# Projection's input turned by VectorE and transfers, overlapping columns of local exponentials added by GpSimd, a new time table

## The reference, cut to what matters

```python
x = x + _layernorm(_L0_attn_ref(_layernorm(x), w_qkv, w_out, b_out))
x = x + _layernorm(_L0_ffn_ref(_layernorm(x), w_freq_real, w_freq_imag, bias))

def _L0_attn_ref(x, w_qkv, w_out, b_out):          # x (2, 8192, 512), 16 heads of 32, W = 64
    qkv = (x @ w_qkv).reshape(B, N, 3, H, Dh)
    # local: query q sees keys from q - 32 to q + 31; softmax over these; times v
    # global: all queries see the keys k[:, ::64] (128 of them); softmax; times v[:, ::64]
    return (out_local + out_global).reshape(B, N, C) @ w_out + b_out

def _L0_ffn_ref(x, w_freq_real, w_freq_imag, bias):
    y = real(ifft(fft(x) @ w))                     # the kernel makes one 512x512 matrix of it
    return y + bias
```

## Time and profile before

| | |
|---|---|
| time, median of 3 runs | 3613.41 us (3602.11 to 3613.45) |
| the profiled execution | 3610.1 us, its span 3608.4 us |
| mean granted clock of TensorE | 0.988 of full speed |
| busy: PE, PEld, DVE, ACT, POOL | 98%, 76%, 63%, 55%, 54% of the span |
| DMA | 571 MB, 158 GB/s over the span |

### The profile page before, as it was taken

One profiled execution on the slowest core, in us unless ns is written; L12 is line 12 of the kernel. 1 busy time (PEld: TensorE's weight loads), 2 busy tenths in 40 slices (PEclk: granted clock), 3 DMA queues, 4 the chain that ended last, 5 costly groups with the idle time before them and its releaser, 6 DMA issues.

```text
span 3608.4 us, 77520 instructions
## 1 busy us (share of the span) xinstructions
PE 3540.8 (98%) x28482; PEld 2753.2 (76%) x28482; DVE 2262.6 (63%) x4672; ACT 1977.4 (55%) x4132; POOL 1935.8 (54%) x3091
## 2 busy tenths in 40 slices
PE   8999999999999899999999999999999999999997
PEld 6888888888888677777777777777777777777775
DVE  4333333333333477777777777777777777777774
ACT  3222222222222467677667767677777777677764
POOL 0000000000000367787787877887777878887787
PEclk9999999999999699999999999999999999999999
DMA  4545545455457666666666666666666666666651
GB/s 151 210 157 192 188 161 209 163 186 195 154 198 217 132 138 152 159 152 143 156 156 157 155 146 154 160 152 143 153 158 155 150 151 151 161 156 146 151 125 42
DMA packets 420885, 571.22 MB, mean 158 GB/s; under 512 B 41656, under 2 KB 187208, under 8 KB 420568
## 3 DMA queue, kind: packets, MB, share of 16 engines
q1 hardware_dynamic: 412024, 564.79, 59.9%
q10 hardware_dynamic: 8256, 2.16, 0.3%
q0 software_dynamic: 288, 0.08, 0.0%
HBM read 361.59 MB, written 203.23 MB: 157 GB/s over the span
## 4 chain that ended last, share of the span: by engine, by line
PE 62%; POOL 1%; ACTq 0%; ACT 0%; issue 0%; DVE 0%; DMA 0%; POOLq 0%; SPq 0%; DVEq 0%
PE ps_misc L1058 19%; PE ps_sc L998 7%; PE ps_ml L974 7%; PE ps_o L1030 6%; PE ps_mg L979 5%; PE ps_s L1030 4%; PE ps_sc L1012 4%; PE ps_o L1042 3%; PE ps_s L1036 3%; PE ps_sc L1067 2%; PE ps_sc L985 1%; PE ps_sc L1006 1%; ACTq L841 0%; POOL rsb L751 0%; DMA w_both<-mt 0%
## 5 line engine op out<-in xcount | busy, mean ns | idle before, releaser
L886 DVE TENSOR_REDUCE mx<-ps_ml 128x2 f32<-128x384 f32 x1024 | 561.7, 549 | 390.8 <-PE ps_ml L974 390.0
L451 PE MATMUL po<-ht_hi,w_both 128*128 128x512 f32 x2048 | 654.2, 393 | 1.5 <-ACT ht_hi L276 1.5
L846 ACT ACTIVATE ps_ml<-mask 128x384 f32<-128x384 bf16 x1022 | 501.9, 491 | 206.3 <-DVE mx L886 128.7
L818 ACT ACTIVATE qk<-ps_sc 128x384 f32<-128x384 f32 (+1 forms) x1024 | 416.8, 458 | 221.0 <-PE ps_sc L998 219.2
L451 PEld LDWEIGHTS po<-ht_hi,w_both 128*128 128x128 f32 x2048 | 385.2, 188 | 81.1 <-ACT ht_hi L276 1.8
L760 POOL TENSOR_SCALAR_AFFINE_SELECT qk<-qk 128x512 f32<-128x512 f32 (+1 forms) x512 | 298.2, 582 | 247.1 <-ACT qk L818 246.1
L889 DVE TENSOR_REDUCE mx<-ps_mg 128x2 f32<-128x256 f32 x1024 | 425.2, 415 | 1.9 <-PE ps_mg L979 1.9
L451 PE MATMUL po<-ht_lo,w_both 128*128 128x512 f32 x1024 | 399.3, 390 | 0.0
L831 ACT ACTIVATE v<-ps_sc 128x512 f32<-128x512 f32 x512 | 304.8, 596 | 94.1 <-PE ps_sc L1012 88.5
L763 POOL TENSOR_SCALAR_AFFINE_SELECT qk<-qk 128x512 f32<-128x512 f32 x512 | 326.0, 637 | 35.0
L455 PE MATMUL po<-w_both,ht_hi 128*128 128x512 f32 x1024 | 332.7, 396 | 0.0
(11 more groups left out here) (161 smaller groups left out, 8194.4 us busy)
## 6 DMA issues: line engine op xcount, KB each, us to landing
w_both<-q_hi_d SPq DMA_DIRECT2D x256, 256.0 KB
ks<-k_hi_d SPq DMA_DIRECT2D x128, 288.0 KB
xb<-in_L_attn_x SPq DMA_DIRECT2D x132, 256.0 KB, 2.9
q_lo_d<-o_lo SPq DMA_DIRECT2D x32, 1024.0 KB, 8.7
k_lo_d<-o_lo SPq DMA_DIRECT2D x32, 1024.0 KB, 10.1
w_both<-q_lo_d SPq DMA_DIRECT2D x128, 256.0 KB
vw<-v_d SPq DMA_DIRECT2D x128, 256.0 KB, 3.0
out<-xb SPq DMA_DIRECT2D x128, 256.0 KB, 3.3
```

What stands on the lines that cost most here:

```text
L451: last = nc.tensor.matmul(po[o % 6][:], wa[:, k, o * P:(o + 1) * P], ha[u][:, k, :], start=start, stop=stop)
L818: nc.scalar.activation(p_loc[:, i, 2 * hp:2 * hp + 2, lo:MW], ps_sc[n % 2][:, 0:2 * MW].rearrange("p (h n) -> p h n", h=2)[:, :, lo:MW], A ...
L846: nc.scalar.activation(ps_ml[u % 2][:, :, 0:MW], mask[:].rearrange("p (o n) -> p o n", o=1).to_broadcast([P, 2, MW]), ACT.Copy).then_inc(s ...
L886: nc.vector.tensor_reduce(mx[s % 2][:, 0, heads, tile], ps_ml[u % 2][:, :, 0:MW], axis=AX.X, op=ALU.max).then_inc(ml_taken, 1)
```

## The change

In the projection, from the second chunk on, TensorE turns nothing any more. VectorE turns the 32x32 blocks of each normalized tile (`turn`) into `turned`, which uses the buffer `at`; 16 transfers issued by ScalarE ahead of output 3 (`move`, `MOVE` = 3), each from 32 partitions to 32 partitions and 64 KB in pieces of 512 B, bring the blocks to their places in `x_t`, which uses `bt`; ScalarE and VectorE split this ahead of outputs 7 and 8 (`split`). To make the blocks land in order, the tokens of a chunk are loaded interleaved (`load_x`, four transfers of 256 KB and not one of 1 MB). The outputs use eight PSUM banks in turn (`bank`) and not six. The first chunk is turned as before.

In the attention, GpSimd adds the last 64 queries of tile i - 1 and the first 64 of tile i for i = 1, 2, 3 into `p_sum`, each after its select. The products with ones are then made in `pvl` 1, 3 and 4 alone: for the columns that one tile fills from `p_loc`, for the others from `p_sum`. The local exponentials wait for the last product of their pair of tiles. The products with the values stay as they are. The numbers of the table are new, and `SEED` has eight values that differ.

```diff
@@ -75,6 +75,10 @@
...
+    BANKS = 8
+    BLOCKS = P // DH
+    MOVES = BLOCKS * BLOCKS
+    MOVE, SPLIT = 3, (7, 8)
...
@@ -96,8 +100,9 @@
...
-        pt = [ctx.enter_context(nc.psum_tensor(f"pt{i}", [P, KT, P], F32)) for i in range(2)]
-        po = [ctx.enter_context(nc.psum_tensor(f"po{i}", [P, D], F32)) for i in range(6)]
+        po = [ctx.enter_context(nc.psum_tensor(f"po{i}", [P, D], F32)) for i in range(BANKS)]
+        pt = [p[:].rearrange("p (a n) -> p a n", a=KT) for p in po[BANKS - 2:]]
+        turned, x_t = at[:].rearrange("p k (b t i) -> p (k b) t i", b=BLOCKS, t=TILES), bt
...
@@ -119,9 +124,12 @@
...
-        banks = [*(p[:].rearrange("p a n -> p (a n)") for p in pt), *(p[:] for p in po)]
...
+        banks = [p[:] for p in po]
...
+        bank = lambda o, u: (o + u * (NOUT + TILES)) % BANKS
+        x_rows = x.rearrange("b n d -> (b n) d")
...
@@ -143,6 +151,12 @@
...
+                def load_x(c, u):
+
+                    for a in range(BLOCKS):
+                        sp.dma_start(xb[u][a * DH:(a + 1) * DH, :, :],
+                                     x_rows[bass.ds(c * CHUNK + a * P, P), :].rearrange("(t i) d -> i t d", i=DH)).then_inc(x_loaded[u], 16)
+
...
@@ -176,9 +190,11 @@
                 def body(c, u, follow):
                     if follow == 2:
-                        sp.wait_ge(t_done, c * TILES + TILES)
-                        sp.dma_start(xb[u][:], x_v[:, bass.ds((c + 2) * TILES, TILES), :]).then_inc(x_loaded[u], 16)
-
+                        if isinstance(c, int) and c == 0:
+                            sp.wait_ge(t_done, TILES)
+                        else:
+                            sp.wait_ge(turn_done, c * TILES)
+                        load_x(c + 2, u)
                     sp.wait_ge(ev_act, c * (NOUT + TILES) + NOUT + TILES)
                     sp.wait_ge(ev_dve, c * NOUT + NOUT)
                     pad_at = c * CHUNK + (c // CPB) * (PSEQ - SEQ) + HALF
@@ -268,12 +284,26 @@
...
-                def t_evac(c, u, t):
-
-                    act.wait_ge(t_done, c * TILES + t + 1)
-                    if t == 0:
+                def first_hi(t):
+
+                    act.wait_ge(t_done, t + 1)
+                    nc.scalar.activation(ht_hi[0][:, :, t * P:(t + 1) * P], pt[t % 2], ACT.Copy).then_inc(t_hi, 1)
+
+                def move(c):
+
+                    act.wait_ge(turn_done, c * TILES)
+                    act.wait_ge(t_lo, c * TILES)
+                    for a in range(BLOCKS):
+                        for b in range(BLOCKS):
+                            act.dma_start(x_t[b * DH:(b + 1) * DH, :, a * P:(a + 1) * P],
+                                          turned[a * DH:(a + 1) * DH, b::BLOCKS, :, :].rearrange("j k t i -> j k (t i)")).then_inc(moved, 16)
+
+                def split(c, u, k):
+
+                    if k == 0:
+                        act.wait_ge(moved, c * (16 * MOVES))
                         at_least(act, mm_done, NOUT + TILES, c, -(NOUT + TILES))
-                    nc.scalar.activation(ht_hi[u][:, :, t * P:(t + 1) * P], pt[t % 2][:], ACT.Copy).then_inc(t_hi, 1)
+                    nc.scalar.activation(ht_hi[u][:, k, :], x_t[:, k, :], ACT.Copy).then_inc(t_hi, 1)
                 def body(c, u, follow):
@@ -281,11 +311,14 @@
                         act.wait_ge(stored[u], (c // 2) * 80)
                         act.wait_ge(kg_copied, c * 2 - 2)
                     for o in range(NOUT + TILES):
-                        if follow and o % 3 == 2:
-                            t_evac(c + 1, 1 - u, o // 3)
+                        if follow and o == MOVE:
+                            move(c + 1)
+                        if follow and o in SPLIT:
+                            split(c + 1, 1 - u, 2 * o - 2 * SPLIT[0])
+                            split(c + 1, 1 - u, 2 * o - 2 * SPLIT[0] + 1)
                         act.wait_ge(mm_done, c * (NOUT + TILES) + o + 1)
                         dst = o_hi[u][:, o, :] if o < NOUT else o_v[u][:, o - NOUT, :]
-                        nc.scalar.activation(dst, po[o % 6][:], ACT.Copy).then_inc(ev_act, 1)
+                        nc.scalar.activation(dst, po[bank(o, u)][:], ACT.Copy).then_inc(ev_act, 1)
                         if isinstance(c, int) and c == 0 and o < KT:
                             piece(2 * KT + o)
@@ -343,13 +376,23 @@
...
-                def t_evac(c, u, t):
-
-                    dve.wait_ge(t_hi, c * TILES + t + 1)
-                    if t == 0:
+                def first_lo(t):
+
+                    dve.wait_ge(t_hi, t + 1)
+                    nc.vector.tensor_tensor(ht_lo[0][:, :, t * P:(t + 1) * P], pt[t % 2], ht_hi[0][:, :, t * P:(t + 1) * P].bitcast(F32),
+                                            ALU.subtract).then_inc(t_lo, 1)
+
+                def turn(c, u, t):
+
+                    dve.wait_ge(xn_done, c * TILES + t + 1)
+                    nc.vector.transpose(turned[:, :, t, :], xb[u][:, t, :].rearrange("p (b i) -> p b i", i=DH)).then_inc(turn_done, 1)
+
+                def split(c, u, k):
+
+                    dve.wait_ge(t_hi, c * TILES + k + 1)
+                    if k == 0:
...
-                    nc.vector.tensor_tensor(ht_lo[u][:, :, t * P:(t + 1) * P], pt[t % 2][:],
-                                            ht_hi[u][:, :, t * P:(t + 1) * P].bitcast(F32), ALU.subtract).then_inc(t_lo, 1)
+                    nc.vector.tensor_tensor(ht_lo[u][:, k, :], x_t[:, k, :], ht_hi[u][:, k, :].bitcast(F32), ALU.subtract).then_inc(t_lo, 1)
...
@@ -367,17 +410,21 @@
                 def body(c, u, follow):
                     if follow:
+                        norm(c + 1, 1 - u, 0)
                         for t in range(TILES):
-                            norm(c + 1, 1 - u, t)
+                            if t + 1 < TILES:
+                                norm(c + 1, 1 - u, t + 1)
+                            turn(c + 1, 1 - u, t)
...
                         dve.wait_ge(stored[u], (c // 2) * 80)
                         dve.wait_ge(kg_copied, c * 2 - 2)
                     for o in range(NOUT + TILES):
-                        if follow and o % 3 == 2:
-                            t_evac(c + 1, 1 - u, o // 3)
+                        if follow and o in SPLIT:
+                            split(c + 1, 1 - u, 2 * o - 2 * SPLIT[0])
+                            split(c + 1, 1 - u, 2 * o - 2 * SPLIT[0] + 1)
                         if o < NOUT:
                             dve.wait_ge(ev_act, c * (NOUT + TILES) + o + 1)
-                            nc.vector.tensor_tensor(o_lo[u][:, o, :], po[o % 6][:], o_hi[u][:, o, :].bitcast(F32),
+                            nc.vector.tensor_tensor(o_lo[u][:, o, :], po[bank(o, u)][:], o_hi[u][:, o, :].bitcast(F32),
                                                     ALU.subtract).then_inc(ev_dve, 1)
...
@@ -424,11 +471,12 @@
...
-                def transposes(c, u, t):
-                    pe.wait_ge(xn_done, c * TILES + t + 1)
-                    at_least(pe, t_lo, TILES, c, t - 1)
+                def transposes(t):
+                    pe.wait_ge(xn_done, t + 1)
+                    if t > 1:
+                        pe.wait_ge(t_lo, t - 1)
...
-                        last = nc.tensor.transpose(pt[t % 2][:, k, :], xb[u][:, t, k * P:(k + 1) * P], ident[:])
+                        last = nc.tensor.transpose(pt[t % 2][:, k, :], xb[0][:, t, k * P:(k + 1) * P], ident[:])
...
@@ -438,8 +486,8 @@
...
-                        p = (o - 6) % (NOUT + TILES)
-                        off = 0 if o >= 6 else -1
+                        p = (o - BANKS) % (NOUT + TILES)
+                        off = 0 if o >= BANKS else -1
...
@@ -448,19 +496,16 @@
...
-                                    last = nc.tensor.matmul(po[o % 6][:], wa[:, k, o * P:(o + 1) * P], ha[u][:, k, :],
+                                    last = nc.tensor.matmul(po[bank(o, u)][:], wa[:, k, o * P:(o + 1) * P], ha[u][:, k, :],
...
-                                    last = nc.tensor.matmul(po[o % 6][:], ha[u][:, k, t * P:(t + 1) * P],
+                                    last = nc.tensor.matmul(po[bank(o, u)][:], ha[u][:, k, t * P:(t + 1) * P],
...
-                        if follow and o % 3 == 1:
-                            transposes(c + 1, 1 - u, o // 3)
-
...
-                        transposes(0, 0, t)
+                        transposes(t)
...
@@ -595,6 +640,7 @@
...
+        p_sum = qk0[:].rearrange("p a n -> p (a n)")[:, 16 * MW:16 * MW + 12 * WIN].bitcast(F32).rearrange("p (i h n) -> p i h n", i=3, h=4)
...
-        MAXIMA = (-12.805, -11.6121, -10.9287, -9.5739, -8.6889, -7.4926, -6.9092, -5.6717)
...
-        SEED = (0.7311, 0.7311, 0.7311, 0.7311, 0.7311, 0.7311, 0.7311, 0.7311)
-        SCORES = (("mt", 0, -4.1303), ("loc", 0, -0.7012), ("loc", 1, 0.756), ("loc", 2, 1.2851), ("loc", 3, 4.7272),
...
-        VALUES = (("pvl", 0, 3.7999), ("pvl", 1, 3.8198), ("pvl", 2, 6.7674), ("pvl", 3, 7.039), ("pvl", 4, 7.8708),
...
```

(42 more changed lines are left out.)

35 lines of the change are left out of this document (18 added, 17 removed).

## The result

3583.67 us, median of 6 runs (3579.64 to 3591.01), against 3612.97 us before (6 runs): 0.9924 of it, 95% interval 0.9908 to 0.9940. That is 29 us less, where 61 were forecast (3552 us). The profiled execution took 3585.8 us, with a span of 3584.1 us.

A forecast was written before the change was run, and what follows sets the result against it. TensorE was taken to bound both long stages. From 3610.1 us, 59 us less for the projection's transposes and 0 for the attention gave 3551, or 3554 from the median; stated 3552 us, with a range of 3508 to 3618.

The forecast's parts named there:

- What bounds the kernel: Both long stages: TensorE, busy in 98% of the span, sets the end; GpSimd has 2.73 us of waits per attention step.
- The transposes, 59 us: Projection: TensorE's transposes leave all chunks but the first, 31 x 1.9 = 59 us less, if delivery precedes the next chunk.
- The issues: Projection: ScalarE issues 16 transfers per chunk at 0.565 us each, 9.0 us, done at 17.2 us, at no cost.
- the 1.05 MB: Projection: extra transfer traffic per chunk, at 80 us of engine time per MB, 5.3 us on 16 engines, landing by 24.
- The 4.6 us in hand: Projection: turned tiles split and ready at 28 us into a chunk, needed at 32.6, so the move costs 0.
- TensorE's shorter sums, 0.24 us per step: Attention: products with ones fall from 1.32 to 1.08 us per step, 31 us over 128 steps; bounds nothing to 42 us.
- GpSimd's add, 0.70 us plus 0.1: Attention: each of three adds per step costs 0.70 us plus a 0.1 gap, 2.4 us, making GpSimd's own work 18.06.
- the attention's period, 18.39 us: Attention: leftover waits keep the step 0.24 us above TensorE's 18.15, the present period, giving back the 31 us; net 0.
- the rival "GpSimd sets the step": Attention: GpSimd's 18.06 us plus remaining waits set the step; with half the waits left, 3685 us in all; chance 22%.
- the point from which it decides: Attention: a step of 18.85 us, or 0.79 us of GpSimd waits, at which the projection's 59 us are used up.
- The table, 0: Attention order: new numbers move items by tenths of a unit, remove no work; 0, up to 20 us of range downwards.
- The rule for the add: Attention: the skill advises VectorE for two-input adds, GpSimd being about twice as slow; on VectorE about 1.1 us for three.

The follow-up runs named there:

- experiment 4: Changed projection, table as before: shorter sums without GpSimd's adds, 3508.83 us; three adds made and waited for but unused, sums as before, 3588.69 us.
- `MOVE` = 4: Changed projection with the attention and table of before, its 16 transfers issued ahead of output 4 instead of 3: 3546.91 us, against 3555.17.
- experiment 7: Changed projection, attention and table of before, transfers issued ahead of output 4 or 5: 3546.91 and 3549.36 us, against 3555.17 ahead of output 3.
- experiment 6: Changed projection, shorter sums, table as before: adds on VectorE 4056.21 us; instead only the small constant's addition there 3549.48; also a deviation operation, transfers later, 3649.34.
- the repaired kernel: The whole change with the table as before, the small constant added on VectorE, and transfers issued ahead of output 4: 3542.95 us.
- the one that leaves the idea out: Changed projection with transfers issued ahead of output 4, attention and table as before the change: 3546.91 us.

## Why the prediction was wrong, by its own steps

- **What bounds the kernel: right.** TensorE sets both stages before. With its part shortened and GpSimd's left alone (experiment 4) the step is 18.06 us, shorter by what the columns taken out come to.
- **The transposes, 59 us: right in the mechanism, 54 to 56 measured.** Some 0.15 us per chunk is lost at the chunk's start, and without it (`MOVE` = 4) the projection's last product stands 60.8 us earlier than before. Two terms under it were off. The issues take 0.96 us each and not 0.565, 15.4 us and not 9.0, since they fall among the stores (experiment 7); the forecast took the median of rows that reach to 1.584; and the 1.05 MB cost 90 us of engine time per MB, not 80 (the page's row of ScalarE's queue is now 34.70 MB at 5.4% of 16 engines). So the pieces are there at 28.7 us after the chunk's start and not at 24, all is split at 32.6 and not at 28. The 4.6 us in hand were not there with the transfers where they stood. That the 59 us came out all the same was luck: the last piece was split 4.6 us later than forecast, and the room was 4.6 us.
- **TensorE's shorter sums, 0.24 us per step: too small.** 0.33 measured, the upper bound by columns. I priced a group of 192 columns by one that another of its kind follows, 0.32 us; the next such group, which other work follows, took 0.44 (2405.70 to 2406.14 in the timeline). That this is the difference is likely, but no run singles it out.
- **GpSimd's add, 0.70 us plus 0.1: right**, 0.733 us and about 0.08. GpSimd's own work per step: 18.06 forecast, 18.04 measured.
- **The step that failed: the attention's period, 18.39 us.** "I expect some to stay: 0.24 us per step above TensorE's own". 0.58 us above it: 18.64, 128 x 0.25 = 31 us, of the 32 that the forecast missed. I treated GpSimd's 2.73 us of waits as room that an add could fill for nothing until it was full, and put the leftover at a value that made the sum zero. What the runs showed in its place: with the old table, the kernel with the adds takes 3588 us and the one without them 3509, and the runs with none to three unused adds show that each costs 7 to 14 us from the first one on, while GpSimd still has waits. The outcome is the rival "GpSimd sets the step", below the point from which it decides (0.6 us of waits stay, 0.79 would have taken it all). For the change itself the split is less sure: no run has the new table with the shorter sums and without the adds, and of the 39.6 us that TensorE waits there 21.6 are the table's wait for ScalarE.
- **The table, 0: wrong as a rule, small in the sum.** By itself it costs 44 us; beside the adds it gives 5, which isn't clear of the spread. Two of its numbers make 38 us, a cost without the adds and a gain with them.
- **The change of stages and its clock: no term at all.** The prediction has the granted clock at 1.00 in both stages and gives the stretch between them no price. In the change it kept its length, by luck; in other kernels it came out between 8 us shorter and 23 us longer.
- **The rule for the add.** The Trainium skill ("GPSIMD Engine Reference", Engine selection) would have the adds on VectorE. GpSimd's load is indeed where the gain went, but the one run with the adds on VectorE was 468 us slower than with them on GpSimd; moving three tiny operations instead brought 39 us.

What stays open: how much of the 4056 us is the place that I gave the adds on VectorE; by which loops the first add's 13 us come, since the wait for the store is there with two and three adds only; and what keeps the clock down between the stages.

## What to carry to other kernels

Idle time of the second engine in a fixed order isn't free room: price each us that it gets by a run with the work made and not used, before counting on it. Where one engine's saving is paid with another's time, add both engines' own work per period first, and look for the smallest thing to take off the second one; three operations of 0.2 us in a step of 18.6 were worth 39 us here. And compare the repaired kernel with the one that leaves the idea out: here they were 4 us apart. An order's numbers are tuned to one load, so compare tables only with the work that they were made for.

## What the runs showed of the hardware

Issuing a transfer of 64 KB in 128 pieces from ScalarE took from 0.59 to 3.1 us here, median 0.62; 16 in a row took 15.4 us beside SP's five stores of 1 MB, and 10.8 us when they began 5.4 us later. An add of 128x256 with both inputs in SBUF took VectorE 0.42 to 1.75 us, median 0.48 (experiment 6), and GpSimd 0.734 us with hardly any spread (0.721 to 0.743). TensorE's granted clock was 1.00 in both long stages of the change (2.4 GHz) and 0.50 (1.2 GHz) in some stretches of 10 us between them, as from 1130 to 1150 us, behind one of 10 us in which TensorE was busy for 6.4; how long it took to come back differed from kernel to kernel.
